# Output projection of the token attentions: from one fp32 matmul to three fp32r passes with a high and a low part

## The reference, cut to what matters

```
q, k, v = split(shift(x) @ wqkv)      # 128 -> 3 x 512, 8 heads of 64
q, k    = rotary(l2norm(q), l2norm(k))
o       = softmax(windowed q k^T) v   # windows of 64, local attention
x       = x + o @ wo                  # 512 -> 128, the projection that is changed
h       = layernorm(shift(x)) @ w1 + b1
x       = x + (a * gelu(g)) @ w2 + b2
```

## Time and profile before

| | |
|---|---|
| median of 3 executions | 1765.33 us (1762.49 to 1766.63) |
| the profiled execution | 1770.82 us, span 1769.0 us, mean granted TensorE clock 0.989 |
| PE busy / weight loads | 1683.6 us (95%) / 1093.5 us (62%) |
| VectorE / ScalarE / GpSimd busy | 1341.4 (76%) / 1307.5 (74%) / 1121.7 us (63%) |
| projection, L772 | 256 records, 131.8 us busy |
| copies of the attended chunk | ScalarE L922 x120, median 635 ns; VectorE L835 x8, 691 ns |

### The profile page before, as it was taken

One profiled execution on the slowest core, in us unless ns is written; L12 is line 12 of the kernel. 1 busy time (PEld: TensorE's weight loads), 2 busy tenths in 40 slices (PEclk: granted clock), 3 DMA queues, 4 the chain that ended last, 5 costly groups with the idle time before them and its releaser, 6 DMA issues. The chain is left out here.

```text
span 1769.0 us, 43496 instructions
## 1 busy us (share of the span) xinstructions
PE 1683.6 (95%) x15560; PEld 1093.5 (62%) x15560; DVE 1341.4 (76%) x2369; ACT 1307.5 (74%) x4472; POOL 1121.7 (63%) x1012
## 2 busy tenths in 40 slices
PE   8998899999989999998999999899999989999999
PEld 5664677775657777554344444577776557777655
DVE  5555898984778989456788887889885688898654
ACT  5445788887358888745899999788887538888863
POOL 5555899992579999603212221799995278999730
PEclk9999999999999999999899999999999999999999
DMA  3001111103011110202655552211102102110111
GB/s 90 2 2 42 25 32 26 26 20 87 13 39 27 28 28 18 70 1 38 130 92 101 97 96 46 60 26 31 26 20 55 51 1 55 26 32 20 43 31 42
DMA packets 67310, 74.90 MB, mean 42 GB/s; under 512 B 13381, under 2 KB 50969, under 8 KB 65049
## 3 DMA queue, kind: packets, MB, share of 16 engines
q1 hardware_dynamic: 67096, 72.13, 19.2%
HBM read 28.08 MB, written 10.49 MB: 22 GB/s over the span
## 5 line engine op out<-in xcount | busy, mean ns | idle before, releaser
L536 POOL TENSOR_TENSOR rsum<-pa,pb 128x512 f32<-128x512 f32 x256 | 325.6, 1293 | 65.4 <-DVE pa L452 35.2
L908 ACT ACTIVATE ffn_prob<-sc,ffn_nmax 128x128 f32<-128x128 f32 x928 | 327.6, 387 | 4.8 <-DVE ffn_nmax L824 4.8
L993 POOL TENSOR_TENSOR ffn_prob<-ffn_prob,ffn_rden 128x512 f32<-128x512 f32 x256 | 265.6, 1059 | 52.2 <-DVE ffn_rden L839 44.6
L545 POOL TENSOR_TENSOR rsum<-rsum,ffn_rnt 128x512 f32<-128x512 f32 x256 | 261.9, 1045 | 10.8 <-ACT ffn_rnt L930 8.5
L462 DVE TENSOR_TENSOR pb<-proj,tab 128x512 f32<-128x512 f32 x236 | 161.8, 686 | 89.0 <-ACT rn L506 88.5
L908 ACT ACTIVATION_READ_ACCUMULATOR ffn_prob<-sc,ffn_nmax 128x1 f32 x928 | 210.4, 227 | 0.0
L442 PE MATMUL pt<-ident,rsum 128*128 128x128 f32 x960 | 154.0, 283 | 10.0 <-POOL rsum L545 7.3
L824 DVE TENSOR_REDUCE ffn_nmax<-sc 128x4 f32<-128x512 f32 x232 | 148.6, 682 | 12.9 <-PE sc L723 10.0
L442 PEld LDWEIGHTS pt<-ident,rsum 128*128 128x128 f32 x960 | 100.7, 140 | 91.2 <-ACT ffn_ptb L916 70.5
L473 DVE TENSOR_REDUCE ffn_ss<-rn 128x16 f32<-128x1024 f32 x128 | 154.6, 1208 | 0.0
L452 DVE TENSOR_TENSOR pa<-proj,tab 128x512 f32<-128x512 f32 x236 | 150.8, 680 | 0.0
(11 more groups left out here) (322 smaller groups left out, 4318.1 us busy)
## 6 DMA issues: line engine op xcount, KB each, us to landing
ffn_v<-ffn_v SPq DMA_DIRECT2D x128, 128.0 KB, 2.3
column_ks<-qk_parts SPq DMA_DIRECT2D x64, 128.0 KB, 4.1
rn<-Y SPq DMA_DIRECT2D x32, 128.0 KB, 2.3
qk_parts<-column_hi SPq DMA_DIRECT2D x64, 64.0 KB, 1.6
qk_parts<-column_lo SPq DMA_DIRECT2D x64, 64.0 KB, 1.6
column_qs<-qk_parts SPq DMA_DIRECT2D x32, 128.0 KB
column_qs<-qk_parts SPq DMA_DIRECT2D x64, 64.0 KB
rn<-Y SPq DMA_DIRECT2D x32, 127.5 KB, 2.4
```

Source lines behind the costliest of these rows:

```text
L536: pool.tensor_tensor(K.sm[:, r, w], K.m1[:, r, w], K.m2[:, r, w], ALU.add).then_inc(S.f_sum, 1)
L545: pool.tensor_tensor(heads(K.sm[:, r, w]), heads(K.sm[:, r, w]), K.rnt[:, r, w * HEADS:(w + 1) * HEADS].unsqueeze(2).broadcast_to([P, HEAD ...
L908: ins = act.activation(K.prob[:, r, e, k], score_banks(i)[e][:, tokens(k)], ACT.Exp, bias=K.nmax[:, r, e, k:k + 1], accum_out=K.den[:, r, ...
L993: pool.tensor_tensor(K.prob[:, r, e], K.prob[:, r, e], K.rden[:, r, e].unsqueeze(2).broadcast_to([P, 4, P]), ALU.mult).then_inc(S.f_pn, 1)
```

## The change

The projection becomes split. ScalarE's copy (in the last two steps VectorE's) rounds the attended chunk into the high part `K.ghi`; a new VectorE instruction, `keep_low`, subtracts it from `ob` into the low part `K.glo`. `f_ot` is now signalled by `keep_low`, and the copy signals a new semaphore `f_oh`. `K.ghi` and `K.glo` exist already for the gated part and have two buffers, where `K.ot` had four. In steps 1 to 27 `keep_low(i - 1)` stands behind the copy of the keys in VectorE's queue; in steps 29 to 31 it stands behind the copy of the probabilities, ahead of the maxima. The weights are split by GpSimd: for `n` = 0 and 2 in step -2, for the others in the gated part of the layer before. Their DMA has the same size and another destination.

```diff
+def output_stage(K):
+    return K.stage[:, 6 * INNER:7 * INNER].rearrange("p (c n) -> p c n", n=P)
...
-    sp.dma_start(K.wo[:], d["L0_ffn_wo"][l].rearrange("(c p) n -> p c n", p=P)).then_inc(S.wa_wo, 16)
+    sp.dma_start(output_stage(K), d["L0_ffn_wo"][l].rearrange("(c p) n -> p c n", p=P)).then_inc(S.wa_wo, 16)
...
+def split_output_weights(pool, K, n):
+    S = K.s
+    pool.wait_ge(S.wa_wo, 16 * (n + 1))
+    pool.tensor_copy(K.wo_hi[:], output_stage(K)).then_inc(S.wo_hi, 1)
+    pool.wait_ge(S.wo_hi, n + 1)
+    pool.tensor_tensor(K.wo_lo[:], output_stage(K), K.wo_hi[:].bitcast(F32), ALU.subtract).then_inc(S.wo_lo, 1)
...
# TensorE, values and project
+            if m == 4:
+                pe.wait_ge(S.wo_lo, n + 1)
...
-            if i == 0:
-                pe.wait_ge(S.wa_wo, 16 * (n + 1))
...
-            pe.matmul(K.ss[:], K.wo[:, c], K.ot[:, c], start=(c == 0), stop=(c == CHUNKS - 1)).then_inc(S.f_wo, 1)
+            pe.matmul(K.ss[:], K.wo_hi[:, c], K.ghi[:, i % 2], start=(c == 0), stop=False)
+            pe.matmul(K.ss[:], K.wo_lo[:, c], K.ghi[:, i % 2], start=False, stop=False)
+            pe.matmul(K.ss[:], K.wo_hi[:, c], K.glo[:, i % 2], start=False, stop=(c == CHUNKS - 1)).then_inc(S.f_wo, 1)
...
# VectorE
-            dve.wait_ge(S.f_wo, TILES * n + i - 3)
-            dve.tensor_copy(K.ot[:, i % 4], K.ob[:]).then_inc(S.f_ot, 1)
+            dve.wait_ge(S.f_wo, TILES * n + i - 1)
+            dve.tensor_copy(K.ghi[:, i % 2], K.ob[:]).then_inc(S.f_oh, 1)
+
+        def keep_low(i):
+            dve.wait_ge(S.f_oh, TILES * n + i + 1)
+            dve.tensor_tensor(K.glo[:, i % 2], K.ob[:], K.ghi[:, i % 2].bitcast(F32), ALU.subtract).then_inc(S.f_ot, 1)
...
+            if LATE + 1 < i < TILES:
+                keep_low(i - 2)
             if i == TILES - 1:
                 keep_output(i - 1)
+                keep_low(i - 1)
             if i == TILES:
                 gate_normal(dve, K, n, 0)
                 keep_output(i - 1)
+                keep_low(i - 1)
...
+            if 1 <= i <= LATE:
+                keep_low(i - 1)
             if i % 4 == 1 and i >= 5:
                 residual((i - 5) // 4)
...
# ScalarE
-            act.copy(K.ot[:, i % 4], K.ob[:]).then_inc(S.f_ot, 1)
+            act.copy(K.ghi[:, i % 2], K.ob[:]).then_inc(S.f_oh, 1)
...
# GpSimd, attention_programs and gated_programs
+            if begin < 0 and i == -2:
+                split_output_weights(pool, K, n)
...
             split_value_weights(pool, K, n + 1)
+            split_output_weights(pool, K, n + 1)
```

More of the change, by code:

```diff
@@ L919, in keep_output @@
             act.wait_ge(S.f_pv, TILES * n + i + 1)
-            if i >= 4:
-                act.wait_ge(S.f_wo, TILES * n + i - 3)
-            act.copy(K.ot[:, i % 4], K.ob[:]).then_inc(S.f_ot, 1)
+            if i >= 2:
+                act.wait_ge(S.f_wo, TILES * n + i - 1)
+            act.copy(K.ghi[:, i % 2], K.ob[:]).then_inc(S.f_oh, 1)
         def inverse_norms(j):
@@ L2103, in __init__ @@
         self.wa_wo = new("wa_wo")
+        self.wo_hi = new("wo_hi")
+        self.wo_lo = new("wo_lo")
         self.wa_hi = new("wa_hi")
@@ L2135, in __init__ @@
         self.f_pv = new("f_pv")
+        self.f_oh = new("f_oh")
         self.f_ot = new("f_ot")
@@ L2234, in ffn @@
         K.w1_lo = sb("w1_lo", [P, 6 * P], F32R)[:, 0:2 * HID]
-        K.wo = sb("wo", [P, CHUNKS, P])
+        K.wo_hi = sb("wo_hi", [P, CHUNKS, P], F32R)
+        K.wo_lo = sb("wo_lo", [P, CHUNKS, P], F32R)
         K.w2 = sb("w2", [P, 3, P])
@@ L2250, in ffn @@
         K.ptb = sb("ptb", [P, 2, 2, 4, P])
-        K.ot = sb("ot", [P, CHUNKS, PAIR])
         K.m1, K.m2, K.sm = K.pa, K.pb, K.rsum
@@ L2263, in ffn @@
         K.nq, K.nl = (K.ptb[:, r].rearrange("p e k j -> p e (k j)") for r in range(2))
-        K.nr = K.ot[:, 0:2]
+        K.nr = sb("nr", [P, 2, PAIR])
         K.gl, K.u = (x[:, 0].rearrange("p e k j -> p e (k j)") for x in (K.prob, K.ptb))
```

## The result

The changed kernel takes 1804.28 us (median of 4 executions, 1799.48 to 1808.19) against 1764.86 us for the kernel before on the same chip: a ratio of 1.0223, 95% interval 1.0195 to 1.0251. It is 39.4 us slower where 34 were forecast, and 1804 lies within the range of 1774 to 1819. The profiled execution took 1805.34 us with a span of 1803.6.

A forecast was written before the change was run, and what follows sets the result against it. TensorE was taken to bound the full steps, the softmax chain the last ones. Full steps 25.5, last steps 6 and start 2.6 made 34 us: 1765.3 + 34 = 1799 us, range widened to 1774 to 1819.

The forecast's parts named there:

- The place of the cost: Full steps: `f_ot`, freeing bank `ob`, comes from the end of VectorE's step; cycle of four steps 0.98 us longer.
- A: The step in four with values ahead of scores; its values were to begin 0.92 us late, waiting for `keep_low`.
- B: Step after A, scores ahead of values: no VectorE idle time left; attend waits 0.18 us for the copied probabilities.
- C and D: Third and fourth steps of the cycle, scores ahead of values: values 0.17 and 0.12 us late.
- The passes' 0.08 us a projection: TensorE's projection as three passes, 0.78 instead of 0.86 us: 0.32 saved in four steps.
- Rival 1: Full steps: VectorE's slack covers the subtraction, so 10 us are saved: 1755 us, or 1749; chance 0.07.
- Full steps: Steps 1 to 26 of four layers: 0.98 us more per four-step cycle, 25.5 us.
- The last steps: Steps 29 to 31: `keep_low` ahead of the maxima delays the softmax chain, 1.5 us a layer, 6 us.
- The start: Layers 0 and 2: GpSimd's two weight-splitting operations make TensorE wait 1.3 us longer each, 2.6 together.
- 2: Rival for the whole kernel: time the same within 0.2%, 3.5 us; chance 0.04.
- rival 4: `keep_low` costs 0.93 instead of 0.60 us, like the rounding beside GpSimd; VectorE bounds everywhere, 1833 us; chance 0.07.
- rival 3: Full steps: only A's wait remains, 0.3 to 0.6 us a cycle, last steps covered; 1773 to 1781 us; chance 0.10.

The follow-up runs named there:

- passes alone: Against the kernel before: three-pass projection without `keep_low`, copies signal `f_ot`, third pass reuses the high part; 1766.31 us, ratio 1.0000.
- work without the wait: Against passes alone: VectorE operation of `keep_low`'s length added, reading nothing of the attention and delaying no signal; 1768.67 us, ratio 1.0009 to kernel before.
- scores first: Against the changed kernel: scores ahead of the values in every step instead of three of four; 1780.07 us, ratio 1.0079 to kernel before.
- late order: Against scores first: chunk 27's copy and `keep_low` in steps 29 and 30 moved earlier, weights split in step -5; 1777.03 us, ratio 1.0057 to kernel before.
- wait without work: Against passes alone: one-column VectorE copy out of `ob` waits and signals `f_ot` as the subtraction does; 1781.49 us, ratio 1.0080 to kernel before.

## Why the prediction was right

- **The place of the cost** held. The step carried by hand came out like this, from one A to the next: values late by 0.92 and 1.02 predicted, 0.90 measured; `keep_low` 0.69, measured 0.68 and 0.60 from start to start; idle before the maxima of A predicted 1.14, measured 1.12; for the squares 0.5, measured 0.47; cycle 30.58, measured 30.66.
- **That the cycle fits to 0.08 us is in part luck.** The chain had TensorE's steps at 8.14, 7.47, 7.46 and 7.41 us and the next values another 0.10 late; measured are 8.31, 7.35, 7.65 and 7.35. It subtracted four times 0.08 for the cheaper passes, which full steps did not get, and left out the 0.10 that the first pass after a wait costs. Against that it added a wait of 0.18 in B for VectorE's copy of the probabilities, and late values in C and D, none of which came. The two errors nearly cancel. VectorE's missing slack in B, on which the prediction rested, costs at most the 0.08 in C that the work alone shows.
- **One input of that chain was off and did no harm.** The rounding in B was carried with 0.88 us and took 0.34 from start to start (649.76 to 650.10); why is told at the end. The half microsecond so won turned up as idle time before the squares of D (0.68 us instead of about 0.2).
- **The passes' 0.08 us a projection was right as a size and wrong as a gain.** Rival 1 took it for 10 us as soon as the values of A need not wait. The passes alone and the work without the wait are that case, and neither gained. In the changed kernel too, the transposes begin 0.92 us after the first pass, not 0.73 to 0.79 as the signs had it. The step that failed is "if TensorE stayed the bound": busy for 168.00 of 168 us meant that no idle time was drawn, not that TensorE's work alone set the pace. Where TensorE is not held by that bound, in the last steps, the term was too small: 0.25 a layer subtracted, 0.57 to 0.69 measured.
- **Full steps:** 25.5 us predicted. Measured 20 cycles x 1.08 = 21.6 for the five cycles of each layer, 0.35 in one cycle of layer 3, and some more before the first residual addition, where the first `keep_low`s stand: in layers 1 and 3, 1.6 and 1.7 (the distance to the kernel before grows from 7.21 to 8.77 us between layers 0 and 1, from 24.87 to 26.54 between 2 and 3), in layer 0, 1.2 beside GpSimd's part. Taken as 1.2 in layer 2 too, that is 27.6 in all.
- **The last steps** were the term most under-sized: 1.5 a layer predicted, 45.34 - 43.03 = 2.3 measured, 9.2 in all, and 1.5 on top in layer 1 of this profile, with the lower clock. Before the passes' saving it is 1.75 against 45.34 - 42.46 = 2.9. The step found, `keep_low` ahead of the maxima in 29, is there. Missed was the other end of the same rule in step 28. In layer 0 of the changed kernel, step 29 reads

```profile
411.27 0.69 DVE L846 COPY ffn_ptb<-pt 128x512 f32<-128x512 f32 x1 [1.93 <-PE pt L749]
...
412.40 0.69 DVE L855 TENSOR_TENSOR ffn_glo<-ob,ffn_ghi 128x512 fp32r<-128x512 f32 x1 [0.44 <-ACT ffn_ghi L948]
413.01 1.28 DVE L840 TENSOR_REDUCE ffn_nmax<-sc 128x4 f32<-128x512 f32 x2
413.15 0.50 PE L786 MATMUL ss<-ffn_ghi,ffn_wo_hi 128*128 128x512 f32 x1 [0.92 <-DVE ffn_glo L855]
```

  From the copy of the probabilities to the maxima it is 1.74 us where it had been 0.61: 1.13 later, and 1.15 were forecast. The projection's wait of 0.92 us in this step stood at 0.20 before.
- **The start:** 2.6 us predicted for layers 0 and 2 together. GpSimd's two operations stand where they were expected (181.45 to 183.35, 1.9 us), and TensorE waits 2.66 us in layer 0 and 2.67 in layer 2 where it waited 1.38: 1.3 each, as forecast. With the split in step -5 it is 1.37 and 1.38 again. From the beginning of this wait to the first residual addition of layer 0 it is 52.09 us against 49.60 before, 2.5 more, these 1.3 and the 1.2 counted above. In layer 2 it is 52.07 against 48.23, 3.8 more: there the granted clock was 0.83 between 1150 and 1160 us, just behind the wait, and the kernel before had 1.00 throughout; in layer 0 both have such a stretch (0.83 before, 0.85 after, between 185 and 195), and in the kernel before 49.60 against 48.23 is its price, 1.4 us. A longer wait does not bring the lower clock by itself: the kernel with the passes alone has the same 2.68 us wait in layer 2 and took 49.34, at 1.00. So with both at 1.00 in layer 2 the longer wait of 1.3 us costs 1.1 (49.34 against 48.23); taken out of scores first again, by the late order, it gave back 0.4 there, and 1.5 in layer 0, where the stretch of lower clock moved too.
- **The sum:** 27.6 + 9.2 + 2.6 = 39.4 us, which is what the medians show; to the tenth it is chance, since only one execution of each kernel was profiled. The two profiled ones stand 34.6 apart: the changed kernel's lost some 3 us more by its clock in layers 1 and 2, and that of the kernel before, which lies 6 us above its median, is 2.9 and 4.6 us slower ahead of that wait in layer 0 and between layers 1 and 2, where the two kernels do the same. Its granted clock is lower there in part (0.93 against 0.97 in the first 50 us).
- **Rivals:** 2 falls with the ratio, rival 4 with `keep_low`'s 0.60. Of rival 3 the price falls and the mechanism holds: VectorE does catch up, by D, and nothing is handed on to the next A. Its 0.6 a cycle came from subtracting 0.32 for the passes; the wait in A alone costs 1.0. Rival 1's mechanism, enough slack in VectorE, is true for the work and false for the late signal, whose cost no slack of VectorE takes up.
- **Signs that missed:** the wait for the squares was to be under 30 us and is 43.1, most of it outside A. VectorE was to be busy over 95% of a cycle, and 153.53 of 168 us is 91% (the prediction's own 28.7 of 30.58 would be 94%). The small waits of the values in C and D don't show in TensorE's timeline.

## What to carry to other kernels

When the evacuation of a PSUM bank becomes two steps on two engines, price first when the bank's release now comes and which instruction stands behind the waiting matmul; the busy time of the new instruction may be the smaller part, and putting work that doesn't need the bank ahead of the wait bought back nine tenths of it here in full steps. Before counting a gain on an engine that is "100% busy", read the distances between starts and the waits of its weight loads: a bound of a tenth of a microsecond hides in the overlap, and work removed before it brought nothing in full steps here. Idle time of an engine can pay for longer work on that engine (0.09 us a cycle here), but not for a signal that another engine, the one that sets the pace, waits for: in three kernels here it cost its own lateness and 0.10 us, whatever the sender's slack.

## What was not expected of the hardware

VectorE's rounding of 128x512 from SBUF to SBUF took 0.93 us before and 0.42 us after in nearly all full steps, with the same instruction and sizes. GpSimd's timeline at the two roundings of 667.38 and 649.76, the kernel before and the one after:

```profile
666.99 1.04 POOL L993 TENSOR_TENSOR ffn_prob<-ffn_prob,ffn_rden 128x512 f32<-128x512 f32 x1
```

```profile
649.77 1.31 POOL L1019 TENSOR_TENSOR ffn_prob<-ffn_prob,ffn_rden 128x512 f32<-128x512 f32 x1
```

Before, the rounding came 0.39 us into GpSimd's operation and ended at 668.31, 0.28 us after that one's end (668.03). Where it came 0.46 or 0.61 us into such an operation it took 0.86 and 0.71 us, and again ended 0.28 us after that one (the first in all the cycles of the wait without work, the second once in the kernel before): it waits it out. Why it then needs 0.28 and not the 0.42 that it takes alone is open. After, it came just as GpSimd passed from one operation to the next, and now GpSimd's operation took 1.31 us instead of 1.04. Whoever comes first has its way, the other pays. The Trainium skill (SBUF — State Buffer, "Who interferes with whom") says just this of copies and casts in a two-port mode, and that an instruction with at most one SBUF input, outside those modes, does not contend with GpSimd. The trace agrees: `keep_low` took 679 to 692 ns in all 128 places. An edit that moves VectorE by half a microsecond can thus change the price of an instruction that it doesn't touch.

Split passes of 512 columns follow each other after 0.31 us for the first behind 128-column transposes and 0.23 for the others. The Trainium skill (TensorE: Matmul & The Clock Gate, "Wait — 56ns, not 53.3ns?") has 215.7 ns at full clock; no row here reached it (the closest is 0.226 us), and three passes took 0.78 us between transposes where nothing stood in their way.
